# Row-sum reciprocals and VectorE's share of the softmax probabilities moved to PSUM, in a cross-attention and mixture-of-experts kernel

## The reference, cut to what matters

```python
x = x + xattn(layernorm(x), ctx, ctx, Wq, bq, Wk, bk, Wv, bv, Wo, bo)   # x, ctx: (16, 128, 128)
x = x + ffn(layernorm(x), router_w, wv, sv, w, s, w1, s1)

def xattn(Q, K, V, ...):            # per token: 16 heads (h) of 8 numbers, attended to 16 keys (g) of 8 numbers
    Q_, K_, V_ = Q.reshape(B, L, 16, 8) @ Wq + bq, K.reshape(...) @ Wk + bk, V.reshape(...) @ Wv + bv
    scores = einsum('blhk,blgk->blhg', Q_, K_) / 8
    attn = softmax(scores, axis=-1)
    return einsum('blhg,blgv->blhv', attn, V_).reshape(B, L, 16 * 64) @ Wo + bo

def ffn(inputs, ...):               # top 2 of 8 experts per token, gated
    gate, index = top_k(softmax(x @ router_w), 2)
    out = (v * gelu(y)) @ w1        # per chosen expert, 128 -> 512 -> 128, with scales
```

## Time and profile before

| what | us |
|---|---|
| median of 3 runs | 258.57 |
| the three runs | 257.31, 258.57, 261.75 |
| span of the profiled execution, first to last instruction | 255.1 |
| TensorE busy | 221.6 |
| VectorE busy | 182.6 |
| GpSimd busy | 142.8 |
| ScalarE busy | 131.3 |

### The profile page before, as it was taken

One profiled execution on the slowest core, in us unless ns is written; L12 is line 12 of the kernel. 1 busy time (PEld: TensorE's weight loads), 2 busy tenths in 40 slices (PEclk: granted clock), 3 DMA queues, 4 the chain that ended last, 5 costly groups with the idle time before them and its releaser, 6 DMA issues.

```text
span 255.1 us, 6298 instructions
## 1 busy us (share of the span) xinstructions
PE 221.6 (87%) x1823; PEld 212.6 (83%) x1824; DVE 182.6 (72%) x432; ACT 131.3 (51%) x362; POOL 142.8 (56%) x159
## 2 busy tenths in 40 slices
PE   7998999998899797955997989999999999999500
PEld 6996889897889797944996979999999999999400
DVE  2798889899899989998266766655665575666226
ACT  2414655668866864646485535555554555554000
POOL 6956546663599689878673354353544435343400
PEclk9979999999999999996599999999999999999955
DMA  4979999999100000011312011122222122000068
GB/s 124 306 157 427 329 326 391 383 375 377 52 22 14 21 31 23 10 52 44 87 52 55 21 35 46 50 73 57 69 58 57 52 52 57 30 10 29 0 228 266
DMA packets 25517, 30.93 MB, mean 121 GB/s; under 512 B 2652, under 2 KB 16896, under 8 KB 25362
## 3 DMA queue, kind: packets, MB, share of 16 engines
q1 hardware_dynamic: 21708, 25.28, 31.2%
q0 software_dynamic: 2528, 4.77, 6.1%
q10 hardware_dynamic: 1254, 0.55, 0.8%
HBM read 16.26 MB, written 14.79 MB: 122 GB/s over the span
## 4 chain that ended last, share of the span: by engine, by line
PE 65%; DVE 14%; issue 6%; ACT 5%; POOL 4%; DMA 3%; DVEq 1%; SPq 0%; ACTq 0%; POOLq 0%
PE bank L1056 26%; PE bank L1075 12%; PE bank L931 8%; PE bank L978 5%; PE bank L865 3%; DVE pv L325 3%; DMA pv<-expert_out 2%; DVE qk L1197 2%; PE bank L986 2%; ACT w_sb L690 1%; PE bank L1040 1%; PE bank L940 1%; PE bank L909 1%; POOL left_no L591 1%; PE bank L989 1%
## 5 line engine op out<-in xcount | busy, mean ns | idle before, releaser
L608 POOL DMA_INDIRECT expert_out<-yo,xs x39 | 38.5, 987 | 49.9 <-DMA expert_out<-yo,xs 26.5
L325 POOL TENSOR_TENSOR pv<-probs,ctx_sb 128x1408 f32<-128x1408 f32 x14 | 40.1, 2866 | 22.0 <-DVE probs L1248 21.9
L566 POOL DMA_INDIRECT routed<-rows,pos x32 | 36.0, 1126 | 17.1 <-DMA routed<-rows,pos 8.0
L1056 PE MATMUL bank<-xsT,g_tile 128*128 128x128 f32 x312 | 42.9, 282 | 3.0 <-ACT xsT L792 1.8
L1056 PEld LDWEIGHTS bank<-xsT,g_tile 128*128 128x128 f32 x312 | 39.4, 198 | 3.5 <-issue 2.0
L1056 PE MATMUL bank<-xsT,v_tile 128*128 128x128 f32 x312 | 42.1, 279 | 0.0
L1075 PE MATMUL bank<-w_sb,hid 128*128 x312 | 41.4, 276 | 0.0
L1384 DVE TENSOR_TENSOR g_tile<-g_sb,g_scale 128x512 f32 x39 | 26.9, 693 | 17.4 <-PE bank L1056 9.8
L1393 DVE TENSOR_TENSOR hid<-bank,act_sb 128x512 f32<-128x512 f32 x39 | 27.0, 691 | 17.3 <-PE bank L1056 15.4
L1056 PEld LDWEIGHTS bank<-xsT,v_tile 128*128 128x128 f32 x312 | 38.8, 196 | 0.0
L1075 PEld LDWEIGHTS bank<-w_sb,hid 128*128 128x128 f32 x312 | 38.0, 192 | 0.2 <-issue 0.2
(11 more groups left out here) (171 smaller groups left out, 310.9 us busy)
## 6 DMA issues: line engine op xcount, KB each, us to landing
routed<-pad_rows SPq DMA_DIRECT2D x4, 2080.0 KB, 20.4
xs<-routed SPq DMA_DIRECT2D x39, 65.0 KB, 1.8
g_sb<-in_L_ffn_w_dram SPq DMA_DIRECT2D x1, 2048.0 KB, 10.7
g_scale<-in_L_ffn_s_dram SPq DMA_DIRECT2D x1, 2048.0 KB, 15.4
v_sb<-in_L_ffn_wv_dram SPq DMA_DIRECT2D x1, 2048.0 KB, 25.9
pv<-expert_out SPq DMA_DIRECT2D x3, 512.0 KB, 5.0
x_sb<-in_x_dram SPq DMA_DIRECT2D x4, 256.0 KB, 6.2
ctx_sb<-in_ctx_dram SPq DMA_DIRECT2D x4, 256.0 KB, 6.3
```

The lines of the kernel that those rows point to most:

```text
L325: return eng.tensor_tensor(pv[:, b, g0:g1, :, :], probs[:, b, :, g0:g1].rearrange("p h g -> p g h").unsqueeze(3).to_broadcast([P, many, H, ...
L566: pool.indirect_dma_start(out=routed[:, :], out_offset=bass.IndirectOffsetOnAxis(ap=pos[:, m % TOP, m // TOP:m // TOP + 1], axis=0), in_=r ...
L608: pool.indirect_dma_start(out=expert_out[:, :], out_offset=bass.IndirectOffsetOnAxis(ap=xs_i[:, t % XB, P:P + 1], axis=0), in_=yo[:, t % X ...
L1056: mm = nc.tensor.matmul(psum[:, n * P:n * P + P], weights[:, c % 2, n * P:n * P + P], xsT[:, c % 2, :], start=True, stop=True)
```

## The change

Three things move.

- `rowinv`, the reciprocals, goes from SBUF to columns 256 to 287 of PSUM bank 5, 16 for each of two buffers.
- Where GpSimd takes keys 0 to 10, the single multiplication of 256 probabilities becomes two: 176 in place in SBUF (for GpSimd, `p_normed`), then 80 written to PSUM bank 5 (for VectorE, a new semaphore `share_normed`). VectorE's `pv` instruction then reads its weights from PSUM instead of SBUF. For tiles 14 and 15 one multiplication writes all 256 to PSUM.
- Bank 5 is no longer free for query products. All of them go to bank 1, so the product of tile t waits for the `qk` of tile t-1.

```diff
+        rowinv = [bank[5][:, (H + b) * H:(H + b + 1) * H] for b in range(2)]
-        rowinv = sb("rowinv", [P, 2, H])
-        def q_bank(b):
-            return bank[1 + 4 * b]
+        def keys_from(t):
+            return POOL_KEYS if t < POOL_TILES else 0
+        def shares(t):
+            many = H - keys_from(t)
+            return bank[5][:, 0:H * many].rearrange("p (h g) -> p h g", h=H)
-        def values(eng, t, b, g0, g1):
+        def values(eng, t, b, g0, g1, weights):
-                                     probs[:, b, :, g0:g1].rearrange("p h g -> p g h")...
+                                     weights.rearrange("p h g -> p g h")...
@@ TensorE, step
-                        if second_on(t):
-                            pe.wait_ge(qk_ready, t - 1)
-                        elif t == 0:
+                        if first_on(t):
+                            pe.wait_ge(qk_ready, t)
+                        else:
                             pe.wait_ge(setup_dve, 3)
-                        nc.tensor.matmul(q_bank(b)[:, 0:P], ...
+                        nc.tensor.matmul(bank[1][:, 0:P], ...
@@ VectorE, value_share
-                    dve.wait_ge(p_normed, t + 1)
+                    dve.wait_ge(share_normed, t + 1)
@@ VectorE, normalise
-                    v.reciprocal(rowinv[:, b, :], rowsum[:, b, :]).then_inc(inv_ready, 1)
+                    v.reciprocal(rowinv[b], rowsum[:, b, :]).then_inc(inv_ready, 1)
-                    v.tensor_tensor(probs[:, b, :, :], probs[:, b, :, :],
-                                    rowinv[:, b, :].unsqueeze(2).to_broadcast([P, H, H]), ALU.mult).then_inc(p_normed, 1)
+                    start = keys_from(t)
+                    if start:
+                        v.tensor_tensor(probs[:, b, :, 0:start], probs[:, b, :, 0:start],
+                                        rowinv[b].unsqueeze(2).to_broadcast([P, H, start]), ALU.mult).then_inc(p_normed, 1)
+                    v.tensor_tensor(shares(t), probs[:, b, :, start:],
+                                    rowinv[b].unsqueeze(2).to_broadcast([P, H, H - start]), ALU.mult).then_inc(share_normed, 1)
```

More of the change, by code:

```diff
@@ L226, in xattn_moe_kernel @@
         s_psum, max_ready, s_shifted = sem("s_psum"), sem("max_ready"), sem("s_shifted")
-        p_ready, sum_ready, inv_ready, p_normed = (sem(n) for n in ("p_ready", "sum_ready", "inv_ready", "p_normed"))
+        p_ready, sum_ready, inv_ready, p_normed, share_normed = (
+            sem(n) for n in ("p_ready", "sum_ready", "inv_ready", "p_normed", "share_normed"))
         pv_pool, pv_dve = sem("pv_pool"), sem("pv_dve")
@@ L546, in step @@
                             pool.wait_ge(zT_psum, t - 1)
-                        values(pool, t, b, 0, POOL_KEYS).then_inc(pv_pool, 1)
+                        values(pool, t, b, 0, POOL_KEYS, probs[:, b, :, 0:POOL_KEYS]).then_inc(pv_pool, 1)
                     for lag in range(PLACES + 1, PLACES + 1 + G):
@@ L904, in step @@
                         pe.wait_ge(xnT_ready, t + 1)
-                        if second_on(t):
-                            pe.wait_ge(qk_ready, t - 1)
-                        elif t == 0:
+                        if first_on(t):
+                            pe.wait_ge(qk_ready, t)
+                        else:
                             pe.wait_ge(setup_dve, 3)
-                        nc.tensor.matmul(q_bank(b)[:, 0:P], xnT[:, quarter_of(j, -1), :],
+                        nc.tensor.matmul(bank[1][:, 0:P], xnT[:, quarter_of(j, -1), :],
                                          q_proj[:, 0:HD, :].rearrange("p i h -> p (i h)"),
@@ L1233, in value_share @@
                 def value_share(t, first=POOL_KEYS, end=H):
-                    dve.wait_ge(p_normed, t + 1)
+                    dve.wait_ge(share_normed, t + 1)
                     if second_on(t):
                         dve.wait_ge(zT_psum, t - 1)
-                    values(v, t, t % 2, first, end).then_inc(pv_dve, 1)
+                    start = keys_from(t)
+                    values(v, t, t % 2, first, end, shares(t)[:, :, first - start:end - start]).then_inc(pv_dve, 1)
                 def normalise(t):
```

5 lines of the change are left out of this document (3 added, 2 removed).

## The result

The changed kernel took 265.57 us, the median of four runs (263.62 to 269.18), against 258.79 for the kernel before measured with it (257.31 to 261.75). The ratio is 1.0206, 95% interval [1.0129, 1.0284]. The forecast was 259.2 with a range up to 261.2, so it was wrong by 6.4 us. Ratios here leave out executions over 1.5% above the fastest of their kernel and medians don't, so for the kernel before, whose executions spread widely, the two can differ.

A forecast was written before the change was run, and what follows sets the result against it. TensorE was taken to set the pace in mid-attention (5.44 us a step), with GpSimd and VectorE holding each other up at the end. Losses 2.69, gains 2.33, clock +0.25: 258.57 + 0.36 + 0.25 = 259.2 us, range from 257.1 less 0.2 to 261.2.

The forecast's parts named there:

- the two ends of the lock: End of attention: VectorE's `pv` and GpSimd's `left_no` stop holding each other up; `pv` 0.81 us, `left_no` near 0.4.
- the -0.60 us of the prediction: Up to the values of tile 15: -0.48 us on TensorE from GpSimd's earlier work, 0.12 from the 3.02 us `pv`.
- the last projection: End of attention: the value sum of tile 15 sets the end, projection at 119.06 instead of 120.79, -1.73 us.
- +2.69 for the waits: Start: query products in one bank wait for `qk` at tiles 1, 2 and 4; with 0.08 for `normalise`, +2.69 us.
- +0.75 for the clock: Start: idle time before the narrow passes may bring the lower clock earlier or longer, 0 to 1.5 us; half taken.
- the +1.95: Start: tile 1's query product waits for `qk` of tile 0, moving setup products and turn of tile 0 by +1.95 us.
- so nothing absorbs it: Start: VectorE already waited 0.56 us for tile 0's scores, so the +1.95 us passes in full down to tile 4.
- I take half: Start: of at most 1.5 us (3.45 - 1.91, the first turn at the lower clock) half is put, +0.75.
- the slow-start rival: Start: clock falls before the narrow passes, costing 1.5 to 2.0 us and nothing at the end; 260.4 to 260.9, chance 0.22.
- the prediction's own sign of failing as a whole: Clock in the first 25 us or around 120 us differing by more than 3 us of time at half speed.
- the clock at the end: After attention: with the gap before the last projection gone, full clock may return earlier, worth 0 to 1.0 us; -0.5 taken.
- with that gone `xn` is done before the value sum is: Last projection: without GpSimd's 1.95 us lateness at `left_no`, the value sum of tile 15 sets the end; -1.73 us.

The follow-up runs named there:

- a3: Changed kernel again, unchanged, without late signals: 257.56 us against 256.85 for the kernel before, ratio 0.9999.
- b0: Kernel before, unchanged, run again for a second profile: 257.64 us against 256.65 for the same kernel beside it, ratio 1.0108.
- b1: Kernel before, unchanged, one execution for its trace: 256.56 us, where the kernel before had a median of 261.13.
- e3: Changed kernel with 8 idle products put ahead of tile 1's query product, while TensorE waits: 255.27 us against 256.65 for the kernel before, ratio 1.0050.
- a1: Changed kernel again, unchanged, with late signals: 264.32 us against 259.69 for the kernel before, ratio 1.0194.
- F: Comparison without late signals, on the same chip as C, of the changed kernel and e4 with the kernel before, which took 256.85 us.
- B: Comparison with late signals that held the changed kernel and e4, among others; the kernel before took 259.69 us.
- C: Comparison with late signals, on the same chip as F, that held the changed kernel and b1, among others; the kernel before took 261.13 us.
- a2: Changed kernel again, unchanged, with late signals: 266.76 us against 261.13 for the kernel before, ratio 1.0260.
- e4: Kernel before with tile 1's query product in bank 5, all others in bank 1, probabilities in SBUF: ratios 1.0068 (B), 1.0153 (D), 1.0040 (F).
- D: Comparison with late signals that held e4 and e8, among others; the kernel before took 261.53 us.
- e8: Changed kernel with tile 1's query product in bank 5 and a GpSimd memset between second and third of six sends: 260.94 us against 261.53, ratio 1.0123.

## Why the prediction was wrong

**Right: the two ends of the lock.** `pv` of 640 at 0.80 to 0.82 us, the first `left_no` at 0.38 us, no new wait in the steady steps. From the turn of tile 4 to `neg_max` of tile 15 the three traces of the kernel before took 71.84 to 71.88 us and the four of the changed kernel 71.23 to 71.29: the -0.60 us of the prediction, to within 0.03. The indirect DMA that took 1.42 us beside VectorE's `pv` took 1.02 where `pv` now reads PSUM:

```profile
100.52 1.02 POOL L573 DMA_INDIRECT routed<-rows,pos  x1 [0.17 <-issue]
```

By the Trainium skill, "SBUF — State Buffer", section "Who interferes with whom", descriptor generation is inferred not to be held up by a `tensor_tensor`. For these DMAs the measurement decides against that: 1.42 us and, for the second of the six, 3.00 us came down to 1.02 and 0.97. Whether it is the making of the descriptors that is held up, or the reading of `rows` and `pos` from SBUF by the same instruction, no run takes apart.

**Mis-sized: the last projection.** -1.73 was forecast; in a3 the projection of tile 15 is 12.93 us behind `neg_max`, in the earlier trace rows 13.69, so -0.76. The mechanism is right: `zT` follows the value sum at once. But VectorE's first value product stood 0.29 us idle ahead of it ("issue") and began 0.39 us later against `neg_max` than in b0, and the sum took 3.67 us at the lower clock where I had put 3.10, 0.57 more. In b0 it took 3.67 as well, hidden behind GpSimd.

**Mis-sized: the start, in both terms.** +2.69 for the waits and +0.75 for the clock, 3.44, were to be lost by tile 4. Counted from VectorE's first `qk`, its turn began at 29.49, 26.73, 30.23 and 27.97 us in the four traces of the changed kernel, and at 24.22, 25.21 and 23.54 in the three of the kernel before: 28.6 against 24.3 in the mean, 4.3 more.

The waits are 1.7 of these, not 2.69. Tile 0's turn moved by 1.87 us from b1 to e3, near the +1.95, and tiles 2 and 4 lost 0.8 where 0.66 was put. What failed is "so nothing absorbs it". VectorE's wait of 0.56 us for the scores of tile 0, on which that rests, was itself the price of a first turn at the lower clock (3.45 us). In b0 and b1, where this turn took 1.91 us, VectorE did not wait there at all, and of the 1.87 us only 1.0 reached its `neg_max`.

The clock is the other 2.6, where 0.75 was put. The failed step is "I take half", of at most the one turn's 1.5 us: the lower clock also took in work on either side of it. In the profiled execution it lasted about 10 us instead of 3, with 1.64 us in the setup products and 1.71 in the turn, and the start lost 3.6 us to it more than the trace of before had; that is the slow-start rival, above its 1.5 to 2.0. With it came the prediction's own sign of failing as a whole, over 3 us more time at half speed in the first 25 us. It isn't always paid in full: in a1 it was 1.5 us in all (26.73 against e3's 25.22). The clock fell during the wait in the profiled execution, and during the setup products in a3 (the row 14 to 15 us has 0.94, the next 0.50). The Trainium skill, "TensorE: Matmul & The Clock Gate", section "What's actually happening", has the monitor run free of the kernel's start; that the clock of one kernel first fell at 12 to 13, 13 to 14, 14 to 15 and 15 to 16 us in four traces fits that.

**Mis-sized: the clock at the end.** -0.5 was forecast. In a3 the clock is back at 124.1 us, just where the first expert product begins, and stays; in the trace of before it was low until 126 to 127. From the first to the last expert product a3 took 115.4 us and the three traces of the kernel before 117.0 to 117.6, so -1.6 to -2.2 us. The mechanism is right. It is also why a3's comparison, 0.7 us above before, came so near the forecast's 0.63: the start cost about what was forecast, the last projection gave 1.0 us less and the clock at the end 1.1 to 1.7 more. That two misses cancel is luck.

**Missing: signals that come late, and the clock behind them.** No term stood for it, and it is most of the 6.4 us. Without late signals the changed kernel is 0.7 us above before in the medians (F); the forecast was 0.63. With them it is 4.6 (B), 5.6 (C) and 6.8 us (the first measurement) above. The step that failed stands among the gains: "with that gone `xn` is done before the value sum is". I asked what is late next on TensorE and ScalarE after the stalls go, not what a faster GpSimd sets loose: six sends at 1.28 us each with no pause, right where TensorE, ScalarE and VectorE hand over tile 13, the logits and tile 15. The kernel before had a 2 us pause there by its own lock, and its distance grew by 0.9 us only. In the first measurement's trace `neg_max` of tile 15 and the last projection are 15.9 us apart, in a3 12.9: 3.0 us for this place.

More is lost behind it, and no experiment took that part apart. Between the first and last expert product the changed kernel took 120.2 to 122.3 us with late signals and 115.4 without. The granted clock over the span, in 40 slices (9 is 0.9 or more), from the pages of a3 and a2, shows where:

```profile
PEclk9968999999999999996899999999999999999955
```

```profile
PEclk9959799999999999967995799999999999999965
```

In a2 the clock falls once more in the experts (slices 21 and 22, about 140 to 150 us), for about 10 us, and TensorE was idle there for 5.4 us instead of 3.8. It is neither the PSUM part nor the row of six alone: e4, all in SBUF and on time at tile 13, took 120.9 and 123.8 us there in B and D and 117.1 in F, and e8, with the pause, still took 121.8. b1, the one trace of the kernel before with records missing, took 117.1.

**Wrong in the base.** I put 3.5 us around the span. Every later run lists its span: it is 1.7 to 1.9 us, so the profiled execution of before was near its fastest, about 256.9.

**What stays open.** Why a comparison has late signals at all, and which of them starts the idle time in the experts. That records go missing in the same traces suggests that the recording of signals itself is what is overrun, and then part of the 2% is a cost of being profiled. The Trainium skill, "NOTIFIC — the notification-queue block", section "7.1 Overflow: three behaviours, one of which stalls the engine", describes a mode in which a full queue of records stalls the engine that writes them, and gives it as the alternative to a mode that drops records, so that both at once would be two queues. No run here shows either, since every execution here was recorded. A version that keeps two query banks beside the shares in bank 5 has no result, since TensorE's writes to that bank and VectorE's use of it would not be ordered.

## What to carry to other kernels

A stall in one engine can be the pause that others need: before taking it away, list what follows the stalled instruction on its own queue and who hands over what while that runs at full rate. Where a wait on TensorE can't be avoided near the start, keep it busy there or move the buffer of that one tile (tile 1 in bank 5); the wait is cheap, the clock behind it is not. And run the kernel before again in every comparison, on more than one occasion: the median of the same program was 2.2 us below and 1.4 us above it.

## What the hardware did that I had not expected

- TensorE's signals came up to 3.5 us after the product's end, beside the fourth and fifth of GpSimd's six indirect DMAs, in three of six comparisons, with a fifth of the signal records missing; the same programs had 0.04 us in the other three.
- One chip showed both conditions on different occasions (C and F).
- A lower clock in a first turn can vanish in a later wait: 1.5 us in tile 0's turn (before against b1) left 0.7 us at tile 4.
- 16 products of 17 columns took 1.96 us at the full clock and 3.60 at the lower one, though their columns are few.
- A VectorE product with its weights in PSUM started 0.29 us later ("issue") behind a chain of small instructions, where the one that read SBUF had no such row.
